# Pacing GpSimd's gathers by ScalarE's pattern pieces in a two-block graph kernel

## The reference, cut to what matters

```python
h = relu(layernorm(x))
wh = (h @ weight).reshape(n, 4, 32)                 # block 1: attention, 4 heads
e = leaky_relu(parent[:, None] + child[None], 0.2)  # from wh and att_weight
att = softmax(where(adj > 0, e, -9e15), axis=1)
x = x + einsum('njh,jhf->nhf', att, wh)
h = relu(layernorm(x))                              # block 2: message passing
msg = relu((adj @ h) @ W_msg.T + b_msg)
x = x + gru_cell(msg, h)                            # 3 gates, 128 wide
```

## Time and profile before

| | us |
|---|---|
| median of 3 runs | 976.55 |
| lowest, highest | 970.72, 979.77 |
| span of the profiled execution | 1278.8 |
| ScalarE busy in it | 654.5 |
| VectorE busy in it | 744.5 |
| TensorE busy in it | 730.5 |
| GpSimd busy in it | 508.6 |

### The profile page before, as it was taken

The page is one execution under the profiler, slowest core; times in us unless marked ns, Lnnn a source line. Parts: engine busy times, 40 slices in busy tenths (PEclk is TensorE's granted clock), DMA queues, the critical chain, the costliest instruction groups (busy, mean ns, idle before and its releaser), DMA issues.

```text
span 1278.8 us, 12294 instructions
## 1 busy us (share of the span) xinstructions
PE 730.5 (57%) x3331; PEld 439.4 (34%) x3381; DVE 744.5 (58%) x3128; ACT 654.5 (51%) x667; POOL 508.6 (40%) x518
## 2 busy tenths in 40 slices
PE   2665447374764747647372726363736454329987
PEld 1443224142432424324141414141414342106643
DVE  7577438484774847748472819383846451127754
ACT  2767518293774937748381809191923122005532
POOL 3110461433426234262435261727255447730360
PEclk9878767685877768777685767676767577659998
DMA  9999928685977969878684858686810002211121
GB/s 318 421 420 423 415 98 344 263 364 209 418 315 297 377 250 415 324 292 349 269 367 145 359 202 334 236 335 233 328 36 19 26 25 51 52 37 34 53 71 34
DMA packets 55750, 305.51 MB, mean 239 GB/s; under 512 B 13825, under 2 KB 31442, under 8 KB 39296
## 3 DMA queue, kind: packets, MB, share of 16 engines
q1 hardware_dynamic: 27936, 274.74, 52.9%
q0 software_dynamic: 17152, 23.15, 6.7%
q10 hardware_dynamic: 10592, 6.82, 1.8%
HBM read 295.65 MB, written 12.71 MB: 241 GB/s over the span
## 4 chain that ended last, share of the span: by engine, by line
another core or an unknown queue 29%; DVE 27%; PE 20%; ACT 11%; issue 8%; DMA 4%; POOL 1%; ACTq 0%; DVEq 0%; POOLq 0%
ACT ind L666 7%; PE ps L925 4%; DVE cand L1389 3%; DVE list_arena L1565 3%; DMA x<-in_x 2%; PE ps L1137 2%; PE ps L970 1%; DVE rows_in L1505 1%; PE ps L971 1%; PE ps L972 1%; PE ps L1160 1%; PE ps L904 1%; PE ps L1162 1%; PE ps L1161 1%
## 5 line engine op out<-in xcount | busy, mean ns | idle before, releaser
L666 ACT ACTIVATE ind<-adj_in 128x4096 bf16<-128x4096 int32 x128 | 461.8, 3608 | 18.1 <-PE ps L925 6.6
L925 PE MATMUL ps<-ind,bit_w 128*128 128x512 bf16 x993 | 318.2, 460 | 194.2 <-ACT ind L666 161.1
L557 POOL DMA_INDIRECT val<-in_adj,val_idx x144 | 151.7, 1054 | 421.7 <-DVE val_idx L1599 351.0
L925 PEld LDWEIGHTS ps<-ind,bit_w 128*128 128x128 bf16 x1024 | 114.5, 114 | 366.5 <-ACT ind L666 175.1
L1389 DVE MAX8 cand<-ps 128x8 f32<-128x256 f32 x256 | 91.1, 418 | 197.2 <-remote 184.3
L539 POOL DMA_INDIRECT rows_in<-wh_table,idx x180 | 180.9, 1005 | 62.3 <-issue 62.3
L617 POOL DMA_INDIRECT adj_in<-g_table,idx x96 | 93.6, 975 | 105.5 <-PE ps L1139 69.3
L694 ACT COPY pm<-ps 128x32 f32<-128x32 f32 x16 | 3.0, 185 | 233.2 <-remote 232.6
L970 PE MATMUL ps<-rows_in,ident 128*128 128x132 f32 x120 | 37.7, 412 | 59.3 <-DVE rows_in L1505 59.2
L957 PE MATMUL ps<-pm,own 128*128 128x8 f32 x128 | 24.5, 320 | 73.0 <-issue 58.9
L1719 DVE TENSOR_SCALAR adj_in<-iota,edge_row,val 128x128 f32<-128x128 f32 x128 | 34.2, 346 | 47.6 <-remote 33.8
(11 more groups left out here) (299 smaller groups left out, 1586.2 us busy)
## 6 DMA issues: line engine op xcount, KB each, us to landing
adj_in<-in_adj SPq DMA_DIRECT2D x128, 2048.0 KB
wh_table<-rows_in POOLq DMA_DIRECT2D x16, 264.0 KB, 8.5
g_table<-t_buf ACTq DMA_DIRECT2D x16, 256.0 KB
out<-rows_in SPq DMA_DIRECT2D x16, 256.0 KB
rows_in<-wh_table,idx POOLq DMA_INDIRECT x180
val<-in_adj,val_idx POOLq DMA_INDIRECT x144
adj_in<-g_table,idx POOLq DMA_INDIRECT x112
ind<-g_table,idx POOLq DMA_INDIRECT x16
```

The costliest lines, as they stand in the source:

```text
L557: nc.gpsimd.indirect_dma_start(out=val2[:, s, k:k + 1], out_offset=None, in_=adj_values, in_offset=bass.IndirectOffsetOnAxis(ap=val_idx2[: ...
L666: nc.scalar.activation(ind[:, (tile * 2 + half) % IND, :], adj_in[:, slot, 0:b - a].bitcast(I32), ACT.Relu, bias=1.0, scale=-1.0, accum_ou ...
L925: ins = nc.tensor.matmul(o, bit_w[:, b, :], ind[:, (tile * 2 + half) % IND, c0:c0 + HALF], start=False, stop=(b == BITS - 1))
```

## The change

`beat(s, n)` is a count of pattern pieces: 8(s + 1) + 6 + n, at most 128. Each triple of gathers of `rows` and of `values` waits until ScalarE has made that many pieces, as does each group of `scan_rows`. So `rows(s)` is issued in four triples, at pieces 6 and 7 of step s + 1 and at the next two; `values(s - 1)` in three triples at the three after that; the two `scan_rows` after those. `rows(s)` now stands ahead of `values(s - 1)`. In the second block GpSimd waits, from group 2 on, until the sums of the group two before are done (LEAD = 2). Nothing is computed otherwise, and no gather is added or left out.

```diff
+LEAD = 2
...
+                def beat(s, n):
+                    return min(2 * G * (s + 1) + 6 + n, 2 * T)
...
                     for t in range(G):
+                        pool.wait_ge(ind_done, beat(s, t))
                         for k in range(3):
                             nc.gpsimd.indirect_dma_start(
...
                     for k in range(E2):
+                        if k % 3 == 0:
+                            pool.wait_ge(ind_done, beat(s + 1, G + k // 3))
                         nc.gpsimd.indirect_dma_start(
...
                 for s in range(1, NG - 1):
+                    rows(s)
                     values(s - 1)
-                    rows(s)
...
                     if 0 <= s - FIRST_SCAN < SCAN_PRE // 2:
+                        pool.wait_ge(ind_done, beat(s, 7))
                         scan_rows(2 * (s - FIRST_SCAN))
+                        pool.wait_ge(ind_done, beat(s, 8))
                         scan_rows(2 * (s - FIRST_SCAN) + 1)
...
                         n = unit(q, h)
-                        if n >= RING2:
-                            pool.wait_ge(agg2_mm, group_of(n - RING2) + 1)
+                        if q >= LEAD:
+                            pool.wait_ge(agg2_mm, max(q - LEAD, group_of(n - RING2) if n >= RING2 else 0) + 1)
```

## The result

| | kernel before | changed kernel |
|---|---|---|
| median of the runs | 978.16 us (970.72 to 982.25, 4 runs) | 1006.38 us (1003.12 to 1009.75, 4 runs) |
| ratio, 95% interval | | 1.0317 [1.0253, 1.0382] |
| recorded execution: time, span | 1278.8 us span | 1004.46 us, 1002.6 us span |

The two medians are 28 us apart; the ratio, which is taken from the fast runs, makes it 31 us (25 to 37). The forecast was 20.6 us slower, 997 us, with 988 to 1006 as its likeliest range; 1006.38 is just above that. The new recording is 276 us shorter than the one of before, and as long as its kernel's timed runs.

A forecast was written before the change was run, and what follows sets the result against it. The prediction took DMA work to bound the scan and GpSimd's queue the stage to the test. 976.55 + 14.6 (scan's end) + 6 (lead), with 0 for the scan, gave 997 us; range 955 to 1008, likeliest 988 to 1006.

The forecast's parts named there:

- The hidden waits: Waits for something unseen in the first recording, 310 us in scan and second block, taken as absent from timed runs.
- 746 + 68 + 153 = 967: Time without hidden waits: 746 us to the last pattern piece, 68 to the list test, 153 for the second block.
- in bursts of gathers only: Claim that TensorE's counts reach other engines late only while GpSimd issues gathers without a pause.
- Part 1: Gathers of the scan in threes, one triple to a pattern piece: cost 0 in the scan, bound by DMA work.
- the rival that the change does not pace: In the scan, pieces come in runs, triples lag and run together: the profile's waits stay; no chance given.
- the first rival: The hidden waits are in the timed runs too, so the changed kernel gets faster; chance 0.19.
- Part 2: Scan's end: gathers held to the pieces make GpSimd's queue and the list test later, +14.6 us, bounds 9 and 16.
- T: The moment the last pattern piece of the scan ends, put near 746 us for runs without hidden waits.
- Part 3: Second block, lead of two groups: groups 12 to 15 need gathers longer than their period, +6 us, bounds 0 and 8.
- the rival that the end costs less: At the scan's end VectorE's and ScalarE's chain ends last, or some waits go: 976 to 985; within 1% had 0.18.

The follow-up runs named there:

- e1: Changed kernel without the two-group lead: gathers of the scan paced and reordered, second block free as before; 987.8 us, 1.0150 of the kernel before.
- e3: Changed kernel without the lead, with pacing and new order only in scan loops 1 to 11, the last three as before; 975.53 us, 1.0004 of the kernel before.
- e8: Kernel before with a lead of three groups in the second block; 979.3 us, 1.0029 of the kernel before.
- e9: Kernel before with TensorE's two message steps of group 15 moved ahead of its wait for the list test; 975.37 us, 0.9958 of the kernel before.
- e10: Kernel before with the last nine values gathers ahead of group 10's early rows, and group 15's message steps ahead of the test; 973.64 us, 0.9945.
- e4: Changed kernel without the lead, with only scan loops 12 to 14 held to the pieces, earlier loops free in the old order; 987.18 us, 1.0153 of before.
- e7: Kernel before with rows(s) written ahead of values(s - 1), no wait on the pieces, no lead; 983.61 us, 1.0071 of the kernel before.
- e5: Kernel before with a lead of four groups in the second block; 975.45 us, 1.0003 of the kernel before.
- e2: Kernel before with the second block's lead of two groups alone; 987.81 us, 1.0144 of the kernel before.

## Why the prediction was right and where it was wrong

**The hidden waits: the conclusion held, the cause did not.** Adding up what a run needs without them (746 + 68 + 153 = 967) and setting it against the timed runs was the step that gave the right sign. The kernel before recorded again has 758.9 + 69.1 + 152.9 by the same stages. The second and third terms were right within 1.1 us; the first was 13 short in this recording, and 1 to 14 short in all of them. The last piece comes at 747 to 760, and not as soon as the DMA engines' busy time, the start and the last piece's work add up to. What failed is the sentence that TensorE's counts reach others late "in bursts of gathers only". The second recording has the bursts and no late count. The expectation that the changed kernel's span would fall to 990 to 1120 held (1002.6), but not because the pacing breaks up the bursts: the unchanged kernel's span fell as well. The expectations of e1 to e3 rested on the same sentence, and their spans missed by 65 us and more. Why the first recording had the waits stays open: none of the twelve later recordings has them.

The Trainium skill, "NOTIFIC — the notification-queue block", section "The write path", was cited for a block that holds its producers back. No run here shows that block. The recordings of e8, e9 and e10 hold 12294 instructions, as many as the first, and have no hidden wait. So the recording of this program alone is not enough for them; what that page describes is neither shown nor ruled out.

**Part 1, the scan: 0, confirmed within 4 us.** e3 has 1.0004 [0.9969, 1.0038], and in the changed kernel the DMA engines are busy 731 us up to the last piece, where 738 were forecast. The threes are there. Three of the last values in the changed kernel's scan:

```profile
721.79 0.99 POOL L564 DMA_INDIRECT val<-in_adj,val_idx  x1 [1.21 <-ACT ind L675]
...
727.74 0.99 POOL L564 DMA_INDIRECT val<-in_adj,val_idx  x1 [2.35 <-ACT ind L675]
...
732.96 1.51 POOL L564 DMA_INDIRECT val<-in_adj,val_idx  x1 [1.62 <-ACT ind L675]
```

They stand 5 to 6 us apart, one to a piece, so the rival that the change does not pace falls. In the first rival the room for hidden waits hung on the rate of the DMA engines. The Trainium skill, "Perfetto Trace Analysis", section "Roofline", gives some 435 GB/s as the bound of the 16 together. The middle of the scan ran at 402 in the changed kernel's window above, at a share of 1.01, so no reserve of that kind shows here.

**Part 2, the scan's end: 14.6 forecast, 15.0 in the recordings (84.1 - 69.1), 14.9 timed (e4, 9.6 to 20.4).** GpSimd's queue in the changed kernel, T = 754.4, with VectorE's index for `rows(14)` ahead of it:

```profile
739.53 0.17 DVE L1466 SCALAR_TENSOR_TENSOR idx<-valid,edge_j 128x4 int32<-128x4 f32 x1
...
748.11 0.94 POOL L580 DMA_INDIRECT edges_more<-g_table,idx  x1 [0.30 <-issue]
749.35 1.01 POOL L544 DMA_INDIRECT rows_in<-wh_table,idx  x1 [0.30 <-issue]
...
763.71 1.00 POOL L544 DMA_INDIRECT rows_in<-wh_table,idx  x1 [0.30 <-issue]
...
777.82 0.96 POOL L573 DMA_INDIRECT adj_in<-g_table,idx  x1 [0.30 <-issue]
...
783.03 1.23 POOL L553 DMA_INDIRECT adj_in<-wh_table,idx  x1 [0.30 <-issue]
...
813.26 0.17 DVE L1608 TENSOR_TENSOR val_idx<-row_i,idx 128x9 int32<-128x9 int32 x1
...
823.27 1.00 POOL L564 DMA_INDIRECT val<-in_adj,val_idx  x1 [0.30 <-issue]
...
838.38 0.14 DVE L1709 CAST over_i<-over_f 1x1 int32<-1x1 f32 x1
```

The last row of `rows(14)` ends at T + 10.3 (forecast 9.6), `early_rows(8)` begins at T + 23.4 (forecast 21.3), and `rows_of_last` at T + 28.6 (forecast some 26). The last values' index is there at 813.43, 10 us ahead of GpSimd; 7 were forecast. The changed queue is as forecast, within 2.3 us.

What stood on the other side was not, and here the number had luck. I wrote that GpSimd stood idle ahead of `rows_of_last` in the kernel before. That idle time of 18.52 us belonged to the first recording, where the index ended the wait. Undisturbed, GpSimd issues without a pause up to T + 11.7, the same figure by another path. The held pass begins at 749.35, T - 5.0, right behind the two `scan_rows`, where the free one begins at T - 21.2, 16.2 us earlier. `rows_of_last` is 16.9 us later than before, and not 14.6; from there to the test the recording of before took 1.9 us more (57.4 us against 55.5, some gathers took up to 2.1 us), and so the test is 15.0 later. Both misses are near 2 us and go opposite ways.

The 5.5 us of e7 are not a share of these 15. In the changed kernel the index for `rows(14)` is there at 739.70, T - 14.7, and the pass begins 9.7 us after it. So there the held `scan_rows` set it, and by this reading the order costs nothing on top. A kernel with the waits and the old order was not run.

**Part 3, the lead: +6 forecast, +11 in the recordings. This is the step that failed: the term was mis-sized.** The mechanism is the forecast one. GpSimd issues 36 gathers without rest, and the sums of groups 13 to 15 wait for them. TensorE in the changed kernel, group 12's last matmul, then groups 13 to 15:

```profile
951.56 1.02 PE L1148 MATMUL ps<-adj_in 128*128 128x512 f32 x2
...
961.67 1.94 PE L1146 MATMUL ps<-adj_in 128*128 128x128 f32 x8 [2.61 <-DMA adj_in<-g_table,idx]
963.40 1.91 PE L1148 MATMUL ps<-adj_in 128*128 128x512 f32 x2
...
973.45 1.16 PE L1146 MATMUL ps<-adj_in 128*128 128x128 f32 x8 [1.61 <-DMA adj_in<-g_table,idx]
974.45 1.02 PE L1148 MATMUL ps<-adj_in 128*128 128x512 f32 x2
...
985.54 1.91 PE L1146 MATMUL ps<-adj_in 128*128 128x128 f32 x8 [3.58 <-DMA adj_in<-g_table,idx]
987.24 1.92 PE L1148 MATMUL ps<-adj_in 128*128 128x512 f32 x2
```

And the first and the last of the 36 gathers:

```profile
935.52 1.00 POOL L626 DMA_INDIRECT adj_in<-g_table,idx  x1 [2.37 <-PE ps L1148]
...
981.64 0.94 POOL L626 DMA_INDIRECT adj_in<-g_table,idx  x1 [0.31 <-issue]
```

From the end of group 10's sums, 0.3 us ahead of that first gather, to the end of group 15's, 989.2, are 53.9 us. The forecast had 49.1: 45 of issue, 2.2 to the landing, 1.9 of sums. Measured are 47.3 to the end of issue (some gathers take 1.2 to 1.4 us where I counted 0.95), 3.0 to the landing, and 3.6 of sums, since after this wait TensorE's matmuls took 1.9 us, where the same matmuls of group 14 took 1.2 and 1.0. The other side was sized too high: five periods of 8.7 are 43.4, but only those of groups 11 and 12 are 8.7; the last three are 8.23 without the lead, so it is 42.0. The difference is 11.9 against 5.7. I had read the period at the middle groups, where it is the same in both recordings, and taken it for the last ones. The bound of 8 that I had set was too low for the same reasons. e5 and e8 agree with the mechanism: with more store the loss goes.

**The sum.** By the recordings 15.0 + 11.2 = 26 us; timed 28 by the medians, 31 (25 to 37) by the ratio. The forecast of 997 us came out 9 us low: 5 of them are part 3, 1.6 are the kernel before, whose median is 978.16 with a fourth run and not 976.55, and the rest lies within the noise. The first rival (faster) falls with e3 and with the second recording, and the rival that the end costs less falls with e4.

## What to carry to other kernels

Before pricing a change against waits that the profile does not explain, compare the recording's span with the timed runs. If it is far longer, as here, record the kernel again before using any of its idle times as sizes; here they belonged to that recording alone. An engine's issue queue is a resource like any other. A wait put into it was free in the middle of this scan, where the engine would have waited anyway, and cost nearly its full length at the end, where the queue itself leads to the next stage. Where gathers may run ahead of their reader, find the groups whose issue takes longer than their use: the lead must carry over all of them together. Here four such groups cost 9.7 us with a lead of two, 1.3 with three and nothing with four. And read a period at the place where it is used: 8.7 us held for the groups in the middle and not for the last.

## What the runs showed of the hardware

- One execution of a program ran with waits of up to 26 us, for something that the profile does not show, behind work that TensorE had ended, by the prediction's estimate 310 us in all. Another of the same kernel had none.
- TensorE began on a gather of 128 x 128 numbers 2.2 to 3.0 us after the end of its last issue (group 15: 982.58 to 985.54) in the changed kernel. VectorE began on gathered values, one number a row, 1.4 us after theirs. The sizes and the readers differ; no run takes them apart.
- TensorE's granted clock was at its lower level for some sums behind a wait for a gather, and the length of the wait alone does not tell which. In the changed kernel, behind waits of 2.61 and 3.58 us the two last matmuls of 128 x 512 took 1.91 and 1.92 us; behind one of 1.61 us, and without a wait, 1.02. But in e2 they took 1.02 behind a wait of the same 2.61 us, and 1.91 behind one of 3.87; and the changed kernel's first sums kept the pace of 1.02 behind 3.01 us. The windows of the changed kernel over the matmuls behind 2.61 and behind 1.61 us, and below them that of e2 behind 2.61 (us, TensorE's busy us, granted clock, DMA share, GB/s):

```profile
961.60:965.40 3.80, 3.73 (x11) 0.55 0.23 62
973.40:975.60 2.20, 2.15 (x11) 1.00 0.45 102
```

```profile
948.30:950.40 2.10, 2.07 (x11) 1.00 0.27 76
```

  0.55 is little more than the lower level, 1.2 GHz, and 1.00 the upper one, 2.4 GHz. At the lower one these sums took 3.6 us (961.67 to 965.31, 985.54 to 989.16), at the upper one 2.0 (973.45 to 975.47).
